# Moving a transposed update one unit later in a software-pipelined mixture of experts

## The reference, cut to what matters

```
def _L1_ffn(x):                                   # x: the layer normalised input of the layer
    xn = (x - mu) * rsqrt(var + EPS) * ln_gamma + ln_beta
    abel_out = gelu(xn @ abel_w + abel_b)
    logits = xn @ moe_gate_w + moe_gate_b
    topw, topi = top_k(logits, 2); topw = softmax(topw)
    w_dense = sum(one_hot(topi, 8) * topw)
    h = gelu(einsum(xn, ew1) + eb1)               # 8 experts, 128 -> 256
    eo = einsum(h, ew2) + eb2                     # 256 -> 128
    moe_out = einsum(eo, w_dense)
    for i in range(3): moe_out = moe_out @ expm(gens[i])
    gate = sigmoid(concat([abel_out, moe_out]) @ gc_w + gc_b)
    return x + abel_out * (1 - gate) + moe_out * gate

x = x + 0.5 * _L1_ffn(layernorm(x))               # before and after the attention layer
```

## Time and profile before

| | |
|---|---|
| median of 3 runs | 1009.77 us (1008.24 to 1009.98) |
| the profiled execution | 1007.76 us, span of its instructions 1006.0 us |
| busy share of the span | PE 85%, DVE 71%, ACT 63%, POOL 60% |
| granted TensorE clock, mean | 0.947 |
| experts, first time | from about 305 to 540 us of the span |
| experts, second time | from about 772 to 1003 us of the span |

### The profile page before, as it was taken

The page is one execution under the profiler, slowest core; times in us unless marked ns, Lnnn a source line. Parts: engine busy times, 40 slices in busy tenths (PEclk is TensorE's granted clock), DMA queues, the critical chain, the costliest instruction groups (busy, mean ns, idle before and its releaser), DMA issues.

```text
span 1006.0 us, 14102 instructions
## 1 busy us (share of the span) xinstructions
PE 859.9 (85%) x3862; PEld 460.3 (46%) x3862; DVE 711.1 (71%) x1535; ACT 638.6 (63%) x1153; POOL 604.4 (60%) x610
## 2 busy tenths in 40 slices
PE   7879677767975999999996688888886899999997
PEld 6734333354432444444443355555543344444443
DVE  6945469965563878887863277777786787887774
ACT  3167489967755887778783444444322787778884
POOL 2064675667458766666675254444457766667674
PEclk9999788869997999999997799999997999999999
DMA  8000000000002222211120000000000213223320
GB/s 213 11 1 0 0 0 1 1 1 1 1 0 85 84 86 85 79 48 58 69 84 0 1 1 0 1 1 1 1 1 1 101 69 95 94 94 95 94 95 22
DMA packets 27406, 42.10 MB, mean 42 GB/s; under 512 B 5320, under 2 KB 19036, under 8 KB 27356
## 3 DMA queue, kind: packets, MB, share of 16 engines
q1 hardware_dynamic: 27356, 41.52, 13.0%
HBM read 39.15 MB, written 2.36 MB: 41 GB/s over the span
## 4 chain that ended last, share of the span: by engine, by line
PE 35%; issue 22%; DVE 19%; POOL 14%; ACT 9%; SPq 1%; DVEq 0%; POOLq 0%; DMA 0%; ACTq 0%
PE bank L1478 7%; PE bank L1480 7%; PE bank L1479 7%; POOL arena L810 5%; POOL arena L754 4%; PE bank L1708 3%; DVE arena L1324 3%; ACT bank L1001 3%; POOL rstd L712 2%; DVE arena L1367 1%; DVE arena L1366 1%; DVE stats L1173 1%; PE bank L1678 1%; ACT arena L993 1%; PE bank L1715 1%
## 5 line engine op out<-in xcount | busy, mean ns | idle before, releaser
L790 POOL TENSOR_TENSOR arena<-arena 128x512 f16<-128x512 f32 x256 | 295.3, 1166 | 125.3 <-ACT arena L993 123.5
L1324 DVE TENSOR_TENSOR arena<-bank,arena 128x512 f32<-128x512 f32 x256 | 172.5, 685 | 79.6 <-ACT bank L1001 63.3
L993 ACT ACTIVATE arena<-arena 128x512 f16<-128x512 f32 x256 | 160.8, 628 | 73.8 <-DVE arena L1324 73.7
L1001 ACT ACTIVATE bank<-bank,eb 128x512 f32<-128x512 f32 x256 | 166.8, 656 | 18.9 <-PE bank L1480 18.5
L817 POOL TENSOR_TENSOR arena<-arena 128x512 f32<-128x512 f32 (+1 forms) x24 | 32.7, 1371 | 117.2 <-DVE arena L1442 89.9
L1478 PE MATMUL bank<-arena,ew1hi 128*128 128x512 f16 x256 | 98.5, 385 | 2.0 <-DVE arena L1324 2.0
L1479 PE MATMUL bank<-arena,ew1hi 128*128 128x512 f16 x256 | 98.5, 385 | 0.0
L1480 PE MATMUL bank<-arena,ew1lo 128*128 128x512 f16 x256 | 97.9, 382 | 0.0
L1478 PE MATMUL bank<-arena,ew2hi 128*128 128x512 f16 x256 | 97.3, 380 | 0.1
L1479 PE MATMUL bank<-arena,ew2hi 128*128 128x512 f16 x256 | 97.3, 380 | 0.0
L1480 PE MATMUL bank<-arena,ew2lo 128*128 128x512 f16 x256 | 97.3, 380 | 0.0
(11 more groups left out here) (274 smaller groups left out, 1876.2 us busy)
## 6 DMA issues: line engine op xcount, KB each, us to landing
arena<-wrows SPq DMA_DIRECT2D x64, 512.0 KB, 5.4
X<-in_L_attn_x_dram SPq DMA_DIRECT2D x8, 256.0 KB, 4.3
out_dram<-X SPq DMA_DIRECT2D x8, 256.0 KB, 6.7
arena<-in_L_ffn_ew_dram SPq DMA_DIRECT2D x2, 512.0 KB, 6.4
arena<-in_L_ffn_ew_dram SPq DMA_DIRECT2D x1, 1024.0 KB
wrows<-arena SPq DMA_DIRECT2D x16, 16.0 KB
arena<-in_L_ffn_gens_dram SPq DMA_DIRECT2D x1, 192.0 KB, 2.7
arena<-in_L_ffn_w_gate_dram SPq DMA_DIRECT2D x1, 192.0 KB, 2.9
```

The costliest lines, as they stand in the source:

```text
L790: pool.tensor_tensor(mo.hlo[:, u % 8, :], mo.hw[:, u % 4, :], mo.hhi[:, u % 8, :], ALU.subtract).then_inc(S.hlo, 1)
L993: A(mo.hhi[:, u % 8, :], mo.hw[:, u % 4, :], ACT.Copy).then_inc(S.hhi, 1)
L1001: A(bank[MM1_BANK[u]][:, :], bank[MM1_BANK[u]][:, :], ACT.Gelu, scale=1.0 / WS, bias=eb1[:, u:u + 1]).then_inc(S.gelu, 1)
L1324: TT(mo.hw[:, u % 4, :], bank[MM1_BANK[u]][:, :], mo.wB[:, p, u // EB, :], ALU.mult)\
```

## The change

PE transposes the update of chunk i-1 in unit 13 of the step instead of unit 12, and DVE adds it to X in unit 14 instead of unit 13. In program order that puts the four transposes behind the abel product, behind the first product of unit 13 and behind `second` of unit 7; on DVE the add stands behind the product of unit 14 and the fourth tile update, and before the product of unit 15. Nothing is added or removed.

```
@@ VectorE, experts, step @@
-                        if lag and u == 13:
+                        if lag and u == 14:
                             dve.wait_ge(S.rT, i)
                             dve.wait_ge(S.zadd, i)
                             if first == 0:
@@ TensorE, experts, step @@
-                        if lag and u == 12:
+                        if lag and u == 13:
                             pe.wait_ge(S.r, i)
                             for t in range(TILES):
                                 tok = slice(t * P, (t + 1) * P)
```

## The result

The changed kernel takes 1020.46 us (median of 4 runs, 1017.68 to 1021.72), the kernel before, on the same chip, 1009.00 us (4 runs, 1008.23 to 1009.98). The ratio is 1.0106, 95% interval 1.0088 to 1.0124: slower by 10.7 us, with 8.9 to 12.5 as its interval. The forecast was 9.3 us and 1019.1 us.

What follows compares the result with a forecast made beforehand. PE was taken to bound the kernel through a loop from L1346 to the next L1346. Transposes 2.6 and logits 4.0 (first stage), plus 2.6 (second), gave 9.3 us: 1009.8 + 9.3 = 1019.1 us, range 1014.0 to 1020.8.

Steps and rivals of the forecast that it cites:

- Part 1: Transposes leave PE's unit 12: the abel product still waits there for copy L1384, so the gain is nothing.
- faster: Rival: unit 12's wait really goes because copy L1384 is done early; 13.2 us faster, 996.6 us; chance 0.06.
- Part 2: Transposes enter PE's full unit 13: 0.44 us in each of 12 full steps, 5.3 us.
- Part 3: VectorE adds in unit 14: first stage's product of unit 15 1.97 us late, L996 late, logits wait; second stage nothing.
- the logits term: First stage, PE's gate logits (L1678) wait 0.8 us for copy L996 in five steps: 4.0 us.
- The bounds of this step: Logits wait per step, first stage: 0 if L1337 is not held up, 1.9 us if none of the slack helps.
- only the transposes cost: Rival: VectorE gets its unit 14 tile update in first, logits never wait; 5.3 us, 1015.1 us; chance 0.20.
- More than forecast: Rival: ScalarE's lateness reaches PE in full, 1.9 us at five places; 14.8 us, about 1024.6 us; chance 0.06.
- No change: Rival: the 0.44 us are absorbed because something other than PE sets the loop; 1009.8 us; chance 0.08.
- The tails: Last two steps of each stage, without tile updates: taken at 0, plus or minus 1 us, shared with other queues.

Runs made afterwards that it cites:

- e4: Kernel before with PE's transposes and abel product both in unit 13, add still in unit 13: 999.72 us, ratio 0.9904.
- e1: Kernel before with only PE's transposes moved to unit 13, VectorE's add still in unit 13: 1014.22 us, ratio 1.0043.
- e8: Kernel before with PE's transposes moved to unit 13 and each of the four done twice, add still in unit 13: 1021.18 us, ratio 1.0106.
- e3: Changed kernel with the first stage's memset and statistics behind the product of unit 15, add still in unit 14: 1013.71 us, ratio 1.0044.
- e7: Changed kernel with the fourth tile update (L1337) in unit 15, behind that unit's product; add and statistics in unit 14: 1013.49 us, ratio 1.0037.
- e5: Changed kernel with PE's abel product moved to unit 13 as well: 1014.76 us, ratio 1.0055.

## Why the prediction was right

The forecast was slower, 1019.1 us; its range, 1014.0 to 1020.8, holds the measured 1020.46 us, near its upper end. The forecast difference of 9.3 us lies within 8.9 to 12.5. Its steps can be checked one by one.

**Part 1, nothing gained in unit 12.** Right. The abel product starts 0.06 us after the copy, as before; the wait only changed its name. e4 is the counter-proof: take the abel product away from that place too and 9.7 us appear. The rival "faster" wanted that wait gone by an early copy; the copy was not early, and it takes the second move to be rid of it.

**Part 2, 0.44 us per full step.** Right in both stages for e1 (0.42 to 0.44) and in the second stage of the whole change, and e8 repeats the price. The intervals of the second stage are 0.42 to 0.45 us longer, all six, together 2.6 us, which is the term of the sum.

**Part 3, late product, late copy, logits wait.** Right as a mechanism; the logits term was mis-sized. I gave 4.0 us for five steps; the trace has 5.0, the difference between after and e1 in the five full intervals of the first stage (7.17 - 2.17 = 5.0). Two things make it up.
- *The logits started later than forecast, above all in the first step.* I forecast 0.8 us per step. Against e1 they start 1.16, 0.80, 0.92, 0.73 and 0.84 us later, 4.45 us together. The product of unit 15 should have started 8.19 us after the moment at which the transposes were free to go; it started 8.48 us after it in the first step (374.75 less 366.27, L1346's end plus 0.05), and 8.12, 8.24, 8.12 and 8.25 in the next four. What differs is DVE's idle time ahead of the statistics, marked `issue`: 0.50, 0.13, 0.26, 0.13, 0.26, 0.13 us in the six full steps, and the intervals follow it: 28.97, 28.60, 28.72, 28.46, 28.57. The forecast of about 28.4 is nearest the steps with 0.13.
- *A group that waits takes longer.* Up to the logits, PE in after and in e1 runs the same pattern to 0.01 us, counted from L1346's start. The logits then start 1.16 us later in the first step, the next matmul 1.26 us later, because the group of eight takes 1.06 us behind a wait and 0.95 without. That is 0.1 us in each of the five steps, 0.5 us together, and 4.45 + 0.5 are the 5.0. (The bracket shows only 1.00 of the 1.26. It counts from the end shown for the matmul before, and the next would have started 0.16 us ahead of that end.)

The extra idle time at the statistics is no work of the change. The kernel before has it in the same steps, inside the group of four, which takes 1.36, 0.99, 1.12, 0.99, 1.12 and 0.99 us in the six full steps. Its first step:

```profile
368.51 0.53 DVE L1173 BATCH_NORM_STATS2 stats<-X  x2
369.34 0.53 DVE L1173 BATCH_NORM_STATS2 stats<-X  x2 [0.30 <-issue]
```

There it cost nothing (27.26 us for this step, 27.27 for the second, which has no surplus). The 1.98 us of the earlier trace rows, on which the forecast of the product rests, were read in the fifth step and hold 0.13 us of it; that is why 8.19 lies between the steps with and without.

The bounds of this step are now measured. The lower one (0) is what e3 and e7 give.

**The rival "only the transposes cost".** It needed DVE to get its tile update in first. L1337 took 1.21 to 1.22 us in all six full steps of the first stage, with POOL recorded 0.02 us ahead each time, so it falls. Yet e3 has the held-up update and still costs only what the transposes do; so the hold-up alone doesn't decide either. It is the sum of the hold-up, the add and the statistics, 3.95 us from product to product, that outruns the slack in front of the logits.

**The other rivals.** "More than forecast" (14.8 us) is out: the logits start at most 1.16 us late, not 1.9. "No change" falls by e1 and e8. The tails changed by -0.3 us together, within the 1 us left for them. What stays open is the 2.1 us ahead of the first full step, which move from execution to execution; why the gap at the statistics is larger in the first, third and fifth full step of the first experts stage; and what decides that POOL goes first in unit 14.

## What to carry to other kernels

When a step is moved to escape a wait, look at what stands behind it on the same in-order queue: if that waits for something later still, the wait only changes its name, and the step is paid in full where it lands, so move both (here both moves gave 9.7 us, where the first alone lost 4.3). Work put ahead of an instruction that feeds another engine costs only what exceeds the slack up to the first consumer that waits, so add up all that stands there, held-up instructions too, before you compare. Once a wait is gone the engine arrives earlier at the next one, and a delay that was cheap grows: the late add cost 6 us beside the transposes alone (after less e1) and 15 beside the faster PE (e5 less e4).

## What the runs showed of the hardware that was not expected

- In unit 14 of the changed kernel POOL was recorded 0.02 us ahead of L1337, and L1337 took 1.22 us in all full steps of both stages. In unit 12 POOL is recorded 0.04 us ahead (0.05 by the rounded starts of the earlier trace rows) in every full step of before and after, and there it goes both ways: L1337 keeps 0.33 us in eight of twelve steps of the kernel before, and takes 1.19 to 1.26 in the other four; in the changed kernel it takes 1.19 to 1.27 in all twelve. The Trainium skill (SBUF — State Buffer, "SBUF: two separate sides") says that whoever starts first keeps the shared port for its whole instruction; the rows agree on the blocking in both places, but the recorded starts don't tell who was first. The held-up updates of unit 12 cost nothing: in the second stage of the kernel before, steps with and without one both take 27.26 us.
- In the first experts stage DVE stood still for 0.13 us between the memset and the first `bn_stats`, in the full steps of before and after. In the first, third and fifth a further 0.37, 0.13 and 0.13 us of idle time were added, in the kernel before inside the group of four, in the changed kernel ahead of it. With the statistics behind the product of unit 15 (e3), the group takes 0.86 us in all six steps.
- A group of eight small matmuls took 1.06 us where it had to wait and 0.95 us where it had not, in all five steps (L1678, first stage, after and e1).
